# High and low expert result rows on two load queues, and the finish in the stacks' memory

## The reference

```python
topk_idx, topk_w = _route(x, gate_weight, e_bias)          # 8 of 64 experts a token
xe = zeros((E, CAP, H)).at[sorted_e, pos].set(tok_sorted, mode='drop')   # CAP = 128 rows an expert
h  = silu(einsum('ech,efh->ecf', xe, w1)) * einsum('ech,efh->ecf', xe, w3)
ye = einsum('ecf,ehf->ech', h, w2)
vals = where(pos < CAP, ye[sorted_e, pos], 0.0)
out = segment_sum(vals * flat_w[:, None], flat_t, num_segments=T)        # 8 rows a token are added
out = out + (silu(x @ shared_gate.T) * (x @ shared_up.T)) @ shared_down.T
x = x + _layernorm(out)
```

## Time and profile before

| | us |
|---|---|
| median of three runs | 1124.87 |
| the profiled execution | 1124.24 |
| its span (first to last instruction) | 1122.4 |
| last scatter issued by POOL | 1059.01 |
| `finish` begins | 1067.05 |
| first matmul on loaded rows | 1071.95 |
| first matmul on the last four-tile piece | 1105.04 |

### The profile page before, as it was taken

One profiled execution on the slowest core, in us unless ns is written; L12 is line 12 of the kernel. 1 busy time (PEld: TensorE's weight loads), 2 busy tenths in 40 slices (PEclk: granted clock), 3 DMA queues, 4 the chain that ended last, 5 costly groups with the idle time before them and its releaser, 6 DMA issues. The chain is left out here.

```text
span 1122.4 us, 16408 instructions
## 1 busy us (share of the span) xinstructions
PE 899.5 (80%) x5114; PEld 290.1 (26%) x5190; DVE 818.8 (73%) x1314; ACT 685.9 (61%) x1416; POOL 559.2 (50%) x729
## 2 busy tenths in 40 slices
PE   6648999999999999999999999999986541736076
PEld 3311222222222222222222222222212221535043
DVE  5788888889889889988988998898831531322057
ACT  5715777777787787777778777777874210323113
POOL 6780020224357455645735655563576754556535
PEclk9868999999999999999999999999998655666589
DMA  5893422012332222222223112000222003410097
GB/s 139 260 256 60 135 60 63 13 40 58 79 101 88 91 96 56 48 50 82 82 89 113 39 40 51 5 6 14 80 87 86 2 3 98 114 44 14 19 393 281
DMA packets 107181, 96.35 MB, mean 86 GB/s; under 512 B 51406, under 2 KB 86512, under 8 KB 105046
## 3 DMA queue, kind: packets, MB, share of 16 engines
q1 hardware_dynamic: 89846, 88.12, 26.0%
q0 software_dynamic: 14336, 4.25, 1.8%
q10 hardware_dynamic: 2912, 2.93, 1.2%
HBM read 49.36 MB, written 65.24 MB: 102 GB/s over the span
## 5 line engine op out<-in xcount | busy, mean ns | idle before, releaser
L269 DVE TENSOR_REDUCE half_max<-s_pair 128x2 f32<-128x1024 f32 x512 | 602.1, 1218 | 76.2 <-PE s_pair L258 69.5
L1423 ACT ACTIVATE probs<-st_bank 128x512 f32<-128x512 f32 x1024 | 544.1, 602 | 169.1 <-PE st_bank L1519 155.1
L1285 POOL DMA_INDIRECT table<-rows,keys_i x256 | 256.3, 1001 | 181.7 <-PE pv_bank L1528 67.2
L1519 PE MATMUL st_bank<-q_stack,k_stack 98*128 98x512 bf16 (+1 forms) x948 | 303.9, 387 | 19.7 <-ACT probs L1423 10.0
L1528 PE MATMUL pv_bank<-probs,values 128*9 128x512 f32 x2048 | 268.6, 596 | 8.0 <-issue 3.0
L258 PE MATMUL s_pair<-k_stack,q_stack 64*128 64x512 bf16 x1024 | 202.9, 395 | 30.1 <-DVE half_max L269 25.3
L258 PEld LDWEIGHTS s_pair<-k_stack,q_stack 64*128 64x128 bf16 x1024 | 49.2, 93 | 346.0 <-issue 199.9
L1519 PEld LDWEIGHTS st_bank<-q_stack,k_stack 98*128 98x128 bf16 (+1 forms) x1024 | 77.8, 97 | 171.6 <-issue 87.8
L1723 POOL DMA_INDIRECT results<-out,ids x64 | 62.3, 974 | 54.6 <-ACT out L1785 38.8
L1756 DVE TENSOR_TENSOR h<-s_pair,gsig 128x256 f32<-128x256 f32 x16 | 6.8, 425 | 70.2 <-ACT gsig L1777 47.4
L1174 POOL CAST shift<-minus_max 128x16 bf16<-128x16 f32 x32 | 6.5, 203 | 98.8 <-DVE minus_max L275 98.7
(11 more groups left out here) (253 smaller groups left out, 857.6 us busy)
## 6 DMA issues: line engine op xcount, KB each, us to landing
results<-zeros SPq DMA_DIRECT2D x8, 2048.0 KB
choices<-results SPq DMA_DIRECT2D x6, 2048.0 KB, 23.4
table<-blank SPq DMA_DIRECT2D x8, 772.0 KB, 6.8
probs<-table SPq DMA_DIRECT2D x16, 386.0 KB
q_stack<-q_image SPq DMA_DIRECT2D x96, 64.0 KB
k_stack<-k_image SPq DMA_DIRECT2D x96, 64.0 KB
k_image<-k_piece SPq DMA_DIRECT2D x16, 256.0 KB, 3.2
table<-rows,keys_i POOLq DMA_INDIRECT x256
```

The costliest lines, as they stand in the source:

```text
L269: nc.vector.tensor_reduce(halves[:, h:HG:SIDE_HEADS, tile, half], stacks.s_pair[slot % S_SLOTS][:].rearrange("p (s k) -> p s k", s=SIDES), ...
L1285: pool.indirect_dma_start(out=table, out_offset=bass.IndirectOffsetOnAxis(ap=keys_i[c % 2][:, pick:pick + 1], axis=0), in_=rows[c % 2][:, ...
L1423: A.activation(probs[:, s % P_SLOTS, :], st_bank[at % ST_BANKS][:], ACT.Exp).then_inc(bank_free, 1)
L1519: M(bank(at)[:], k_stack[g][own, tile // PER, h, tile % PER * P:(tile % PER + 1) * P], q_stack[g][own, half, h, :], start=True, stop=True) ...
```

## The change

Each token's eight rows are now loaded as two halves: rows 0 to 3 (low) and rows 4 to 7 (high). For each piece there are two loads instead of one, in all 20.

- **High rows** are loaded by SP, at the end of its code in `run_experts`. SP first waits for the scatters of rounds 10 to 14 (`put_of`), for the last up projection (`up_ready`) and for the last down projection (`y_ready`), since the rows go to the memory of the q and k stacks, which hold the expert weights.
- **Low rows** are loaded by ACT. It waits for the scatters of the last round, then issues the loads of pieces 0, 1 and 2 (`LOW_EARLY = 3`) still in `run_experts`. The other seven stand at the head of its code in `finish`. They go to the memory of `probs` (pieces 0 to 4) and to new tensors `low_rows`.
- A half row group is 4 x 512 bytes = 2 KB in a row in DRAM, every 4 KB. Before it was 8 KB (two tiles) or 16 KB (four tiles).
- Both loads of a piece increment one semaphore, and PE and DVE wait for 32 instead of 16.
- `whole` lies in the memory of `xfT`. `finish` runs inside the stacks' context, so that their memory is still held.

The arithmetic of `finish` and its order on PE, DVE and POOL are the same. The core of the diff:

```diff
+PIECES = ([slice(0, PER // 2), slice(PER // 2, PER)] + [slice(c * PER, (c + 1) * PER) for c in range(1, CHUNKS - 1)]
+          + [slice(TILES - PER, TILES - PER // 2), slice(TILES - PER // 2, TILES)])
+LOW = TOPK // 2
+LOW_EARLY = 3
 class ExpertRows:
+        self.high = [whole(a) for a in (q[0], q[1], q[2], q[3], k[0], k[2], k[3], k[1])]
+        self.low = [flat[:, c * PER * LOW * DIM:(c + 1) * PER * LOW * DIM] for c in range(CHUNKS // 2)]
+        self.results_in = [sem(f"results_in{c}") for c in range(len(PIECES))]
+    def place(self, parts, c):
+        first, tiles = PIECES[c].start % PER, PIECES[c].stop - PIECES[c].start
+        return parts[PIECES[c].start // PER].rearrange("p (t k d) -> p t k d", t=PER, k=LOW)[:, first:first + tiles]
+    def load_results(self, engine, results, c, half):
+        engine.dma_start(self.place((self.low, self.high)[half], c).rearrange("p t k d -> p t (k d)"),
+                     results.rearrange("(p t v k) d -> p t v (k d)", p=P, t=TILES, v=2)[:, PIECES[c], half, :]).then_inc(self.results_in[c], 16)
 # run_experts, sync
+            for r in range(ROUNDS - 1 - OUT_DEEP, ROUNDS - 1):
+                put_of(sp, r)
+            sp.wait_ge(up_ready, ROUNDS)
+            sp.wait_ge(y_ready, ROUNDS)
+            for c in range(len(PIECES)):
+                rows_of.load_results(sp, results, c, 1)
 # run_experts, scalar
+            put_of(act, ROUNDS - 1)
+            act.wait_ge(turned, ROUNDS)
+            act.wait_ge(slot_read, 2 * ROUNDS)
+            for c in range(LOW_EARLY):
+                rows_of.load_results(act, results, c, 0)
 # finish
+        rows_of.low += [sb(f"low_rows{c}", [P, PER * LOW * DIM])[:] for c in range(CHUNKS // 2, CHUNKS)]
+        low, high = ([rows_of.place(parts, c) for c in range(len(pieces))] for parts in (rows_of.low, rows_of.high))
+        whole = consts["xfT"][:].rearrange("p (t d) -> p t d", t=TILES)
-            for c in range(len(pieces)):
-                sp.dma_start(rows[c][:].rearrange("p t k d -> p (t k d)"), ...).then_inc(loaded[c], 16)
-                pe.wait_ge(loaded[c], 16)
+                pe.wait_ge(loaded[c], 32)
-                dve.wait_ge(loaded[c], 16)
+                dve.wait_ge(loaded[c], 32)
 # finish, scalar
+            for c in range(LOW_EARLY, len(pieces)):
+                rows_of.load_results(act, results, c, 0)
```

More of the change, by code:

```diff
@@ L125 @@
 Q, DEEP, OUT_DEEP = 4, 7, 5
+PIECES = ([slice(0, PER // 2), slice(PER // 2, PER)] + [slice(c * PER, (c + 1) * PER) for c in range(1, CHUNKS - 1)]
+          + [slice(TILES - PER, TILES - PER // 2), slice(TILES - PER // 2, TILES)])
+LOW = TOPK // 2
+LOW_EARLY = 3
+assert TOPK - LOW >= Q
 class ExpertRows:
@@ L143, in __init__ @@
         self.weights_in = sem("weights_in")
+        q, k = stacks.q, stacks.k
+        self.high = [whole(a) for a in (q[0], q[1], q[2], q[3], k[0], k[2], k[3], k[1])]
[7 more added lines that the diff above has]
+                     results.rearrange("(p t v k) d -> p t v (k d)", p=P, t=TILES, v=2)[:, PIECES[c], half, :]).then_inc(self.results_in[c], 16)
     def load_rows(self, sp, table, r):
@@ L1847, in _, with finish @@
                     turn(r + 3)
-def finish(nc, consts, results, out):
+def finish(nc, consts, rows_of, results, out):
     with ExitStack() as ctx:
@@ L1857, in finish @@
         x1, shared, ident = consts["x1"], consts["shared"], consts["ident"]
-        ADDED = TOPK // 2
-        HALF = PER // 2
-        pieces = [slice(0, HALF), slice(HALF, PER)] + [slice(c * PER, (c + 1) * PER) for c in range(1, CHUNKS - 1)] + [slice(TILES - PER, TILES - HALF), slice(TILES - HALF, TILES)]
+        pieces = PIECES
         size = lambda c: pieces[c].stop - pieces[c].start
         tiles = lambda c: pieces[c]
-        rows = [sb(f"choices{c}", [P, size(c), TOPK, DIM]) for c in range(len(pieces))]
-        whole = sb("whole", [P, TILES, DIM])
+        rows_of.low += [sb(f"low_rows{c}", [P, PER * LOW * DIM])[:] for c in range(CHUNKS // 2, CHUNKS)]
+        low, high = ([rows_of.place(parts, c) for c in range(len(pieces))] for parts in (rows_of.low, rows_of.high))
+        loaded = rows_of.results_in
+        whole = consts["xfT"][:].rearrange("p (t d) -> p t d", t=TILES)
         stats, mv = sb("statsE", [P, TILES, 6]), sb("mvE", [P, TILES, 2])
@@ L1869, in finish @@
         bank = [ctx.enter_context(nc.psum_tensor(f"sum_bank{a}", [P, CHUNK], F32)) for a in range(2)]
-        loaded = [sem(f"loadedE{c}") for c in range(len(pieces))]
         stored = sem("storedE")
@@ L1883, in _ @@
         def _(sp):
-            width = TOPK * DIM
-            for c in range(len(pieces)):
-                sp.dma_start(rows[c][:].rearrange("p t k d -> p (t k d)"),
-                             results.rearrange("(p r) d -> p (r d)", p=P)[:, tiles(c).start * width:tiles(c).stop * width]).then_inc(loaded[c], 16)
             for c in range(len(pieces)):
@@ L1900, in _ @@
                 M(to, ident[:], shared[:, tiles(c), :], start=True, stop=False)
-                pe.wait_ge(loaded[c], 16)
-                for r in range(ADDED, TOPK):
-                    mm = M(to, ident[:], rows[c][:, :, r, :], start=False, stop=(r == TOPK - 1))
+                pe.wait_ge(loaded[c], 32)
+                for r in range(LOW):
+                    mm = M(to, ident[:], high[c][:, :, r, :], start=False, stop=(r == LOW - 1))
                 mm.then_inc(bank_done, 1)
@@ L1910, in sum_and_stats @@
             def sum_and_stats(c):
-                dve.wait_ge(loaded[c], 16)
-                V.tensor_tensor(rows[c][:, :, 0:2, :], rows[c][:, :, 0:2, :], rows[c][:, :, 2:4, :], ALU.add).then_inc(summed, 1)
+                dve.wait_ge(loaded[c], 32)
+                V.tensor_tensor(low[c][:, :, 0:2, :], low[c][:, :, 0:2, :], low[c][:, :, 2:4, :], ALU.add).then_inc(summed, 1)
                 dve.wait_ge(summed, sum_step(c, PAIRS))
-                V.tensor_tensor(whole[:, tiles(c), :], rows[c][:, :, 0, :], rows[c][:, :, 1, :], ALU.add).then_inc(summed, 1)
+                V.tensor_tensor(whole[:, tiles(c), :], low[c][:, :, 0, :], low[c][:, :, 1, :], ALU.add).then_inc(summed, 1)
                 dve.wait_ge(summed, sum_step(c, FOUR))
@@ L1993, in program @@
             run_experts(nc, table, consts, rows_of, results)
-        finish(nc, consts, results, out)
+            finish(nc, consts, rows_of, results, out)
 def shape_constants():
```

## The result

The changed kernel takes 1128.77 us (median of nine runs, 1124.59 to 1132.82) against 1123.36 us for the kernel before (nine runs, 1119.19 to 1125.11). The ratio is 1.0059, 95% interval 1.0040 to 1.0078: 4.5 to 8.8 us slower, clear of the 0.2% that can be told from no change. The forecast was 1125.4 and no measurable change. The profiled execution took 1132.50 us, with a span of 1130.7.

What follows compares the result with a forecast made beforehand. DMA loads thinly bound the finish, PE and DVE close behind. PE 1.4 us earlier and DVE 1.9 late give +0.5: span 1122.9, plus 1.84 outside makes 1124.7, the profiled run 0.63 under the median: 1125.4 us, range 1120.7 to 1129.2.

Steps and rivals of the forecast that it cites:

- The term that failed: ACT's loads in finish: last issue returns with 127 rows an engine outstanding, after 129 low steps, at 1088.0; DVE 1.9 us late.
- The step before it: Before the barrier: low piece 0 starts moving when SP's piece 6 issue returns, at 1063.6; 39 low steps by 1072.5.
- in step with a held SP: Load issues before the barrier: one engine's issue waits while the other's is held, so ACT meets SP stuck at 1061.4.
- The same term at the barrier: SP's ten loads: last issue returns after 129 steps; with low steps, SP ends at 1072.5 and the barrier opens at 1072.7.
- the middle case (limit at 160): SP's loads before the barrier: with a limit of 160 rows, barrier at about 1069 and end near 1122.
- The need of DVE: Finish: DVE wants ACT's normalised piece 0 for residual(0) at 1087.0, with piece 2 coming 7.72 us after PE's start.
- equal shares: Loads in the finish: the high and low queues share the DMA engines, so a low step takes 0.172 us.
- the price of the short rows: All loads: 2 KB rows at 380 GB/s take 44.2 us instead of 38.7, 5.4 us more DMA work.
- pieces no longer waited for: PE in the finish: its idle time before pieces 2 to 7 is gone, spacing 4.43 us.
- A (SP not held): Rival at the barrier: SP's issues are not held, barrier stays at 1067.0, DMA binds, time 1121.2; chance 0.21.
- B (two queues slower than one by far): Rival in the loads: two queues of 2 KB rows get less than one; 6.9 us later at 300 GB/s; chance 0.21 with C.
- C (low behind all high): Rival at piece 0: low rows wait behind high loads issued earlier, PE 3.6 us later, 1129.0; chance 0.21 with B.

Runs made afterwards that it cites:

- e3: Changed kernel, but SP issues five high loads before the barrier and all later loads, low and high, behind it in order of need: 1094.4 us, ratio 0.9962 to before.
- e9: Changed kernel, but SP instead of ACT issues the low loads of pieces 8 and 9, behind the barrier: 1121.54 us, ratio 1.0020 to before.
- e2: Changed kernel, but SP issues five high loads before the barrier and five behind it, ACT's loads unchanged: 1101.6 us, ratio 1.0041 to before.
- e10: As e3, but four instead of five high loads ahead of the barrier: 1114.54 us, ratio 0.9950 to the kernel before.
- e8: As e3, but two instead of five high loads ahead of the barrier: 1094.9 us, ratio 0.9964 to the kernel before.

## Why the prediction was wrong

It had the right wait (ACT held, its first normalisation late, DVE late with it), but the term that gives its length was too small: the return of a held issue, when "at most some 127 rows an engine are outstanding on its queue". A second step, when ACT's rows start to move, was wrong too.

- **The term that failed.** For ACT it gave 256 - 127 = 129 low steps; 158 had moved. In the prediction's count ACT is free at +29.0, measured +34.3: 5.3 later. The forecast end was +63.9, measured +68.7: 4.8 later. The trace splits the 5.3 us into two parts. The low queue had moved 129 steps (4.23 MB) at 1093.1, +31.1, and the 29 steps more took until 1096.24: 3.1 us are the term. The row is its traffic from 1067.28 to 1093.1:

```profile
q10 hardware_dynamic: 2138, 4.22, 44.3%
```

- **The step before it.** The other 2.2 us are a late start of the low rows. The prediction let them move as soon as SP's seventh issue returned, at +4.6. They first moved at +9.2: the last scatter, for which ACT waits as well as POOL, was met at +5.3 instead of +2.4, and from ACT's first issue to its first row 3.8 us went by. At +15.8 the low queue had the 39 steps that the prediction had at +13.5; from there its 90 steps took 15.3 us (forecast 15.5).
- **ACT was not in step with a held SP,** as the prediction read the earlier trace rows. Its three early issues took 1.44 us while SP's eighth was held. The late first row is not SP's hold either. In e3 SP had left its early issues at 1036.4 (its drain at the barrier) and issued nothing more until 1047.6, yet ACT's rows, issued at 1041.83, first moved at about 1045.6, again 3.8 us later:

```profile
L1703 SPq DRAIN  x1: 122/122/122, 1036.4 to 1036.4; - x1
1041.83 1.44 ACTq L170 DMA_DIRECT2D probs<-results  x3
```

- **What e9 shows, and what not.** It gives back 4.2 us by taking 32 rows an engine from ACT, and its end is within 0.6 us of the forecast. That nearness is luck: with 224 rows issued the prediction's rule lets ACT go at 97 steps, (97 - 39) x 0.172 = 10.0 us behind 1072.5, +23.5; it went at 119 steps, +29.7.
- **The same term at the barrier.** SP's last issue returned at 158 steps instead of 129, and the barrier opened at +16.1 instead of +13.7. That cost little while ACT was held: e2 opened it 5 us earlier and ended 0.9 us earlier.
- **Why I had 127.** Both numbers came from one burst of token loads, 32 rows each, of which the first held one returned at 128 and the second at 126. SP's first two held issues in the changed kernel gave 122 and 129. The later ones, held one behind the other, gave less: 119 for 32 rows, 98 for 16. I had no row of a long held train, or of 16-row loads in one, and should have kept the range open on the side of fewer outstanding; the prediction names only the milder side ("the middle case (limit at 160)").
- **The need of DVE** came at 1097.19 - 6.38 = 1090.81, +28.9 (forecast +28.0). It would have been later, since PE started 2.6 us late, but piece 2 began 1085.10 - 1079.22 = 5.9 us behind piece 0 and not 7.72. That is mostly the granted clock, since the gap of 0.82 was already out of the 7.72. Before, PE stood idle for 3.67 us ahead of piece 0, and its clock was at 0.50 (1.2 GHz) until 1077.5, 5.5 us into the pieces; here PE worked from the barrier on, and it was at 0.50 until 1081.5, only 2.3 us in. In both it was then at 1.00. DVE was 6.4 us late and not 1.9.
- **Right:** the rate (380 forecast, 385 to 388 measured); equal shares; the price of the short rows (5.4 and 4.7); pieces no longer waited for (0.75 us in all); SP held and the barrier late.
- **Not seen:** the last scatter lands later beside loads (5.3 us against 2.4). In the changed kernel POOL's drain behind it ends at 1072.8, 5 us before SP, so at the barrier it is hidden; ACT's early loads it made 2.9 us later. In e2, e3 and e10 it sets the barrier at +11.1.
- **The rivals.** A (SP not held) fell with SP's 18.6 us of issues; B (two queues slower than one by far) with 385 GB/s; C (low behind all high) with low piece 0, which landed 8.3 us behind its issue while high pieces issued before it were still moving.

Why an issue in a held train returns so late stays open. Without its own rows, SP's eighth returned with 87 outstanding and its ninth and tenth with 82, as if it looked at the earlier loads alone. Counted so, the 90 held issues (over 1 us) of the change and its variants returned with 67 to 98 outstanding, 72 of them with 72 to 88. But ACT's seventh passed unheld with 107 before it, and its eighth was then held until 72. No run tested a rule.

## What to carry to other kernels

Count the rows, not the bytes, that one engine puts on its load queue. A train of 128 an engine on an empty queue went through ahead of the barrier, but behind it e3's fourth load, which made 128, was held for 2.9 us. No issue here was held with fewer than 82 rows of earlier loads outstanding; above that it may stand still until some 70 to 100 of them are left. So such a train belongs on an engine that nobody waits for, ahead of no barrier and no computation, and in the order of need. When a model has two holds in it, ask which one the end hangs on: here the end hung on ACT's 14 us; an earlier barrier alone gave back 0.9 us, and freeing ACT alone, with the rows out of order, 1.2, where freeing both in the order of need gave 10.8. A threshold read from one burst is a value with one sign of error unknown; carry both signs into the range.

## What the runs showed of the hardware

- Held issues returned, their own rows counted, with 102 to 130 rows an engine outstanding for loads of 32 rows an engine, and with 83 to 102 for loads of 16. Others returned within 0.8 us with up to 148 outstanding (e2, ACT's seventh). Rows of 8 KB count as one: ten loads of 1 or 0.5 MB went through in 5.3 us.
- While SP's issue was held, ACT's issues returned (0.39 to 0.49 us). Their first row moved 3.5 to 3.9 us behind the first issue in the eight traces in which SP's queue still had rows to move all that time, whether SP was held or not; 1.7 us in e10, where that queue ran empty meanwhile, and 1.1 in e8, where it was empty.
- Two queues with rows of unequal length got nearly equal numbers of packets, not of bytes: 359 packets with 2.61 MB against 356 with 0.70 MB in the same 8 us.
- 2 KB rows from DRAM run at 404 GB/s on one queue beside the scatters and 385 to 388 in the finish; 4 to 16 KB rows at 415 to 433.
- An indirect scatter of 128 rows of 512 bytes is met 2.3 to 2.7 us behind its issue on idle DMA engines, and 5.2 to 6.1 us beside loads.
